# Attention over the context: scaled keys, a negated row maximum, and row sums half a slot later

## The chip, the cores and the metric

One core of one Trainium2 chip runs the whole program. The metric is the device time of one execution in microseconds. An execution was also recorded by the hardware profiler; its rows are used below.

## What is computed

A transformer block with an encoder over a short context (2 x 77 tokens) and a decoder over 2 x 2048 tokens in blocks, width 512, 16 heads of 32. What matters here is the decoder's attention over the encoder's output:

```python
q = (xq @ wq.T + bq).reshape(Bq, Tq, H, hd).transpose(0, 2, 1, 3)
k = (xkv @ wk.T + bk).reshape(Bq, Tk, H, hd).transpose(0, 2, 1, 3)
v = (xkv @ wv.T + bv).reshape(Bq, Tk, H, hd).transpose(0, 2, 1, 3)
scores = jnp.einsum('bhqd,bhkd->bhqk', q, k) / jnp.sqrt(jnp.asarray(hd, xq.dtype))
scores = scores + bias[None]
attn = jax.nn.softmax(scores, axis=-1)
out = jnp.einsum('bhqk,bhkd->bhqd', attn, v)
```

The bias depends on the distance of the positions alone and is constant beyond 127, so for most query rows it drops out of the softmax.

## The kernel before

The program runs its stages one after the other: encoder, decoder projections, attention of the decoder over itself, its output with the next projection, `cross_attention` (the attention over the context), feed-forward. Each stage is a block of five instruction streams, one for each engine, ordered by semaphores; the next block starts when all have ended.

In `cross_attention` the queries are worked in chunks: 8 groups of 512 tokens (`GW`) times 4 sets of 4 heads (`KC`, `HC`) are `NQ` = 32 chunks, each of `TT` = 4 blocks of 128 queries. A block has 4 x 77 = 308 columns of scores. Block `n` goes through these steps:

- `score(n)` on TensorE, three matmuls into one of three PSUM banks (`sps`). It waits until the exponentials of block n-3 have freed the bank.
- `shift(n)` on VectorE (L1279): if the block is near (`near(n)`: the first two blocks in the chunks of the first group of each batch, 16 in all) it adds the bias (L1287), then takes the maximum over the 77 columns of each head (L1289, into `mx`) and multiplies by -SCALE (L1291, into `ng`).
- `exponent(n)` on ScalarE (L1243): four activations, one for each head, exp(SCALE * score + ng), into `pq` (L1248).
- `sums(n)` on VectorE (L1293): the row sums into `den` (L1296); `inverse(n)` (L1298) takes the reciprocal for two blocks (L1301).
- GpSimd multiplies `pq` by the reciprocal (L1162).
- For the chunk: `turn` on TensorE transposes `pq` into two PSUM banks (L1198), `evacuate` on ScalarE copies them out (L1256), `values` multiplies with the values (L1208), `high` (ScalarE, L1262) and `low` (VectorE, L1306) split the result in two parts, `project` on TensorE multiplies with the output weights (L1222), and `residual` on VectorE adds `y` (L1311), to which GpSimd has added the bias row (L1169).

The order is written out by hand as slots from -2 to 36. In slot q the engines do the scores, maxima, exponentials and sums of chunk q+2 (`LEAD`), the transposes of chunk q, the values of chunk q-1, `high` and `low` of chunk q-2, and the projection of token block q-5 (`LAG`). A slot has two halves, with two blocks and two transposed heads in each. VectorE's half is: maxima of two blocks, sums of the same two, their reciprocal. ScalarE's half is: two evacuations, then the exponentials of two blocks. In slots 0 to 15 GpSimd also splits a block of weights for a later stage in two parts (L431, L436, L438).

The keys come from the encoder. There, for each of four chunks `m`, TensorE leaves a projection in PSUM and VectorE writes its high part (`ckh`, L405) and what is left (`ckl`, L407). `G` holds the rows of the relative bias; each has its constant far value taken off and is divided by SCALE (L331).

Of the kernel before, what the change touches and what calls it, by code (L numbers as in the profile page):

```python
# [30 lines left out]
P = 128  # L31
# [85 lines left out]
def encoder(k, io, dr, ident, weights):  # L117

    nc = k.nc
    with k:  # L120
# [34 lines left out]
        s = k.sems("enc", "x wqkv wo wff1 wff2 wkv cols vrow grow gx0 gx1 g gs bias gx ones idz id mm xc"  # L155
                          " sq var sd rs hs h qk v st sc mx sub ex sum rec nrm pt ptc ot otc x1 hid mem ck cl cv one out")

# [160 lines left out]
        def _(dve):  # L318
# [10 lines left out]
            dve.wait_ge(s["gx0"], 2)  # L329
            for i, f in ((0, far_sa), (1, far_sa), (2, far_ca), (3, far_ca)):  # L330
                dve.tensor_scalar(G[:, i, :], G[:, i, :], f[:, 0:1], 1.0 / SCALE, ALU.subtract, ALU.mult).then_inc(s["gx1"], 1)  # L331
            dve.wait_ge(s["gx1"], 4)
# [3 lines left out]
            for n, (kind, m) in enumerate(UNITS):  # L336
# [65 lines left out]
                elif kind == "ck":  # L402
                    ready(n)
                    bk = cols[:, BCK + m:BCK + m + 1]
                    dve.tensor_scalar(ckh[:, m, :], out[:, 0:SE], bk, None, ALU.add).then_inc(s["ck"], 1)  # L405
                    dve.wait_ge(s["ck"], m + 1)
                    dve.scalar_tensor_tensor(ckl[:, m, :], out[:, 0:SE], bk, raw(ckh[:, m, :]),  # L407
                                             ALU.add, ALU.subtract).then_inc(s["cl"], 1)
                else:
# [641 lines left out]
def cross_attention(k, io, dr, ident, w, split, src, dst):  # L1051
# [7 lines left out]
    with k:  # L1059
# [3 lines left out]
        ub = k.sb("ca_ub", [P, 2, H, S])  # L1063
        mx = k.sb("ca_mx", [P, PB * TT, HC])
        ng = k.sb("ca_ng", [P, PB * TT, HC])
# [11 lines left out]
        ops = [k.ps(f"ca_p{i}", [P, D]) for i in range(2)]  # L1077
        s = k.sems("ca", "zero0 zero1 key0 key1 val near brow q0 q1 q2 score biased max shift exp sum inverse normal"
                         " turned copied value high low product added done y0 y1 y2 y3 st0 st1 st2 st3")
# [5 lines left out]
        def chunk(q):  # L1085
            return q // KC, q % KC, q // KC // GB

        def blocks(q):
            return [q * TT + i for i in range(TT)]

# [58 lines left out]
        def _(pool):  # L1149
# [7 lines left out]
            for q in slots():  # L1157
                if has(q + LEAD):
                    for n in blocks(q + LEAD):
                        pool.wait_ge(s["inverse"], n // 2 + 1)  # L1160
                        r = n % (PB * TT)
                        pool.tensor_tensor(pq[:, r], pq[:, r], inv[:, r].unsqueeze(2).to_broadcast([P, HC, S]),  # L1162
                                           ALU.mult).then_inc(s["normal"], 1)
# [78 lines left out]
        def _(act):  # L1242
            def exponent(n):  # L1243
# [3 lines left out]
                for j in range(HC):  # L1247
                    last = act.activation(pq[:, r, j, :], sps[n % 3][:, j * S:(j + 1) * S], ACT.Exp,  # L1248
                                          bias=ng[:, r, j:j + 1], scale=SCALE)
                last.then_inc(s["exp"], 1)  # L1250
# [25 lines left out]
        def _(dve):  # L1276
            dve.memset(raw(kd[0][:]), 0.0).then_inc(s["zero0"], 1)

            def shift(n):  # L1279
# [3 lines left out]
                if near(n):  # L1283
# [4 lines left out]
                    dve.wait_ge(s["biased"], nears(n))  # L1288
                dve.tensor_reduce(mx[:, r], tile, AX_X, ALU.max).then_inc(s["max"], 1)  # L1289
                dve.wait_ge(s["max"], n + 1)  # L1290
                dve.tensor_scalar(ng[:, r], mx[:, r], -SCALE, None, ALU.mult).then_inc(s["shift"], 1)  # L1291

# [20 lines left out]
            for q in slots():  # L1313
                if has(q - 2):
                    low(q - 2)
                for half in range(2):
                    if has(q + LEAD):
                        n = TT * (q + LEAD) + 2 * half
                        shift(n)
                        shift(n + 1)  # L1320
                        sums(n)
                        sums(n + 1)
                        inverse(n)
                    if half == 0 and has(q - LAG - 1, NE):
# [481 lines left out]
```

## Time and profile before

| | us |
|---|---|
| median of three runs | 3056.75 |
| lowest and highest | 3056.3, 3058.85 |
| the profiled execution, its own time | 3056.01 |
| its span, first to last instruction | 3054.2 |
| first bias addition of the stage, start | 1968.80 |
| last residual of the stage, start | 2267.24 |

The page of a profile shows for each engine the time it was busy, the span in slices, and a chain of work followed back from the end. Here the core is mostly busy with matmuls, and the stage in question covers about a tenth of the span. Busy shares say little of it: engines wait for each other, so it is read by slots, by waits and by the timeline.

### The profile page before, as it was taken

The page shows a single profiled execution, that of the slowest core. Times are in us where ns is not written, and L with a number is a line of the kernel's source. Part 1 is how long each engine was busy: PE and PEld are TensorE (multiplying, and loading weights), DVE is VectorE, ACT ScalarE, POOL GpSimd, SP SyncE. Part 2 cuts the span into 40 slices and gives each one's busy share as a digit, 9 for nine tenths or more (in the row PEclk, how much of TensorE's full clock was granted, in tenths as well). Part 3 has the DMA queues.
Part 4 walks back from the last instruction along what each step waited for, and adds up shares of the span by engine and source line. Part 5 has one row for each costly group of instructions (what it writes and reads, how often), then busy time and mean ns, then how long its engine had stood idle before and what let it go on. Part 6 is the DMA issues. An engine that isn't in the chain of part 4 may idle for free. (4 is left out here: it accounts for less than half of the span.)

```text
span 3054.2 us, 42604 instructions
## 1 busy us (share of the span) xinstructions
PE 2765.9 (91%) x12704; PEld 1815.9 (59%) x12704; DVE 1662.1 (54%) x3992; ACT 1241.8 (41%) x2630; POOL 373.6 (12%) x459
## 2 busy tenths in 40 slices
PE   5689978999999999999999499588969999999998
PEld 4578864444444444444443377456647777777777
DVE  4244537777777777777774466378842221222211
ACT  0032322555555555555555243276733222222222
POOL 0300002000000000000000111266447000000000
PEclk7899996999999999999999799799989999999999
DMA  9344444222222222222220775534331000000000
GB/s 286 74 164 167 180 162 119 63 64 64 65 64 65 64 65 64 65 66 64 64 64 8 177 234 192 167 114 136 125 113 47 28 28 28 1 27 27 28 14 14
DMA packets 133924, 271.63 MB, mean 89 GB/s; under 512 B 33875, under 2 KB 54867, under 8 KB 128192
## 3 DMA queue, kind: packets, MB, share of 16 engines
q1 hardware_dynamic: 128896, 254.17, 28.6%
q0 software_dynamic: 4800, 14.68, 1.6%
q8 instruction: 111, 1.82, 0.3%
q14 instruction: 117, 0.96, 0.1%
HBM read 174.39 MB, written 99.98 MB: 90 GB/s over the span
## 5 line engine op out<-in xcount | busy, mean ns | idle before, releaser
L969 ACT ACTIVATE sa_pr<-sa_st 128x512 f32<-128x512 f32 (+3 forms) x1280 | 612.1, 532 | 566.4 <-DVE sa_st L1032 324.4
L937 PE MATMUL sa_ov<-sa_pr,sa_v 128*33 128x512 f32 (+3 forms) x2560 | 537.7, 541 | 0.0
L1018 DVE TENSOR_REDUCE sa_part<-sa_mp 128x1 f32<-128x512 f32 (+3 forms) x768 | 411.4, 583 | 120.4 <-PE sa_mp L918 119.5
L928 PE MATMUL sa_st<-sa_q,sa_k 97*128 97x512 f32 (+3 forms) x1280 | 439.8, 413 | 23.8 <-ACT sa_pr L969 13.2
L928 PEld LDWEIGHTS sa_st<-sa_q,sa_k 97*128 97x128 f32 x1280 | 216.9, 190 | 323.1 <-ACT sa_pr L969 206.1
L918 PE MATMUL sa_mp<-sa_k,sa_q 96*128 96x512 f32 (+3 forms) x1280 | 373.5, 386 | 25.2 <-DVE sa_mp L996 19.7
L1015 DVE CUSTOM_DVE_ANT_0 sa_mp<-sa_mp,sa_ub 128x512 f32<-128x512 f32 (+3 forms) x512 | 318.0, 664 | 76.7 <-PE sa_mp L918 71.8
L1676 DVE TENSOR_TENSOR ff_hl<-ff_hf,ff_hh 128x512 fp32r<-128x512 f32 x128 | 93.9, 734 | 479.4 <-ACT ff_hh L1658 479.4
L105 PE MATMUL ff_f<-ff_ln_hi,ff_w 128*128 128x512 f32 x1024 | 344.0, 397 | 2.9 <-DVE ff_ln_lo L529 2.9
L1621 PE MATMUL ff_o<-ff_w,ff_hh 128*128 128x512 f32 x1024 | 323.8, 397 | 3.1 <-DVE ff_hl L1676 3.1
L918 PEld LDWEIGHTS sa_mp<-sa_k,sa_q 96*128 96x128 f32 x1280 | 233.2, 194 | 96.0 <-DVE sa_part L1018 24.4
L1655 ACT ACTIVATE ff_hf<-ff_f,ff_b 128x512 f32<-128x512 f32 x128 | 88.0, 687 | 471.6 <-PE ff_f L105 471.5
L937 PEld LDWEIGHTS sa_ov<-sa_pr,sa_v 128*33 128x33 f32 x2560 | 122.2, 111 | 258.0 <-issue 206.6
L1032 DVE TENSOR_TENSOR sa_st<-sa_st,sa_tb 128x256 f32<-128x256 f32 (+1 forms) x608 | 206.9, 381 | 81.6 <-PE sa_st L928 80.2
L105 PEld LDWEIGHTS ff_f<-ff_ln_hi,ff_w 128*128 128x128 f32 x1024 | 193.5, 189 | 50.5 <-DVE ff_ln_lo L529 3.3
L1621 PEld LDWEIGHTS ff_o<-ff_w,ff_hh 128*128 128x128 f32 x1024 | 191.2, 188 | 51.3 <-DVE ff_hl L1676 3.4
L1428 POOL TENSOR_TENSOR sao_y<-sao_y,sao_brow 128x512 f32<-128x512 f32 x32 | 42.3, 1354 | 1363.5 <-DMA sao_y<-in_x 1363.5
L105 PE MATMUL ff_f<-ff_ln_lo,ff_w 128*128 128x512 f32 x512 | 203.0, 396 | 0.0
L1621 PE MATMUL ff_o<-ff_w,ff_hl 128*128 128x512 f32 x512 | 202.2, 395 | 0.0
L105 PE MATMUL qkv_ring<-ln_hi,qkv_w 128*128 128x512 f32 x512 | 165.0, 397 | 3.4 <-DVE ln_lo L529 3.4
L1248 ACT ACTIVATE ca_pq<-ca_s,ca_ng 128x77 f32<-128x77 f32 x512 | 120.8, 335 | 96.4 <-DVE ca_ng L1291 95.8
L1188 PE MATMUL ca_s<-ca_k,ca_q 128*128 128x308 f32 x384 | 85.6, 346 | 47.9 <-ACT ca_pq L1248 30.6
(186 smaller groups left out, 3361.3 us busy)
## 6 DMA issues: line engine op xcount, KB each, us to landing
sa_q<-scratch_q SPq DMA_DIRECT2D x192, 128.0 KB, 4.4
sa_k<-scratch_k SPq DMA_DIRECT2D x192, 128.0 KB, 4.6
scratch_q<-qkv_qst SPq DMA_DIRECT2D x32, 512.0 KB, 2.8
scratch_k<-qkv_qst SPq DMA_DIRECT2D x32, 512.0 KB, 2.8
scratch_q<-sao_qst SPq DMA_DIRECT2D x32, 512.0 KB, 2.9
ca_q<-scratch_q SPq DMA_DIRECT2D x32, 512.0 KB, 4.1
scratch_v<-qkv_vst SPq DMA_DIRECT2D x8, 1056.0 KB, 5.2
sa_v<-scratch_v SPq DMA_DIRECT2D x16, 528.0 KB, 6.5
```

The lines of the kernel that those rows point to most:

```text
L105: last = pe.matmul(out, s, m, start=(k == 0), stop=(k == n - 1))
L918: pe.matmul(mp[a % 2][:, h, 0:w], qs[n.par][rows, h, qb * P:(qb + 1) * P], ks[n.par][rows, h, k0:k0 + w], start=True, stop=True).then_inc( ...
L928: pe.matmul(st[bank(u, h)][:, 0:w], ks[n.par][:, h, kb * P:(kb + 1) * P], qs[n.par][:, h, g * GW + c0:(g + 1) * GW], start=True, stop=True ...
L937: last = pe.matmul(ov[64 * h:64 * h + VW, c0:GW], vs[n.par][:, kb, h, :], pr[:, u % 4, h, 0:GW - c0], start=(u in opens), stop=(u in ends))
L969: act.activation(pr[:, u % 4, h, 0:w], st[bank(u, h)][:, 0:w], ACT.Exp, scale=SCALE).then_inc(s["exp"], 1)
L1015: dve.tensor_tensor_reduce(tile, tile, ub[n.par][:, h, GW - w:GW], 1.0, NEG, ALU.add, ALU.max, to)\
L1018: dve.tensor_reduce(to, tile, AX_X, ALU.max).then_inc(s["red"], 1)
L1032: dve.tensor_tensor(tile, tile, tb[n.par][:, h, t0:t0 + w], ALU.add).then_inc(s["bias"], 1)
L1248: last = act.activation(pq[:, r, j, :], sps[n % 3][:, j * S:(j + 1) * S], ACT.Exp, bias=ng[:, r, j:j + 1], scale=SCALE)
L1621: last = pe.matmul(ops[i][:], a[:, f % 2, t], b[:, f, :], start=(f == 0 and n == 0), stop=(f == FC - 1 and n == 2))
L1655: act.activation(hf[:, f % 2, :], fps[f % 2][:], ACT.Relu, bias=b1[:, f:f + 1]).then_inc(s["relu"], 1)
L1676: dve.tensor_tensor(hl[:, f % 2, :], hf[:, f % 2, :], raw(hh[:, f % 2, :]), ALU.subtract)\
```

## The change

- In the encoder the projected key plus its bias is multiplied by SCALE in full precision into `sq` (a tile that is free by then), copied into `ckh`, and the difference goes to `ckl`. There is one semaphore more, `cs`.
- The bias rows for the attention over the context are no longer divided by SCALE.
- In `cross_attention` the scores are thus scaled already. The maximum is written with its sign turned (`negate=True`) straight into `ng`; `mx`, its multiplication and its semaphore go. The exponential has no scale.
- VectorE takes the sums and the reciprocal of the two blocks of the half before, and GpSimd's loop over blocks is moved by two blocks with it.

```diff
-            for i, f in ((0, far_sa), (1, far_sa), (2, far_ca), (3, far_ca)):
-                dve.tensor_scalar(G[:, i, :], G[:, i, :], f[:, 0:1], 1.0 / SCALE, ALU.subtract, ALU.mult).then_inc(s["gx1"], 1)
+            for i, f, unit in ((0, far_sa, 1.0 / SCALE), (1, far_sa, 1.0 / SCALE), (2, far_ca, 1.0), (3, far_ca, 1.0)):
+                dve.tensor_scalar(G[:, i, :], G[:, i, :], f[:, 0:1], unit, ALU.subtract, ALU.mult).then_inc(s["gx1"], 1)
...
-                    dve.tensor_scalar(ckh[:, m, :], out[:, 0:SE], bk, None, ALU.add).then_inc(s["ck"], 1)
+                    dve.tensor_scalar(sq[:, m, :], out[:, 0:SE], bk, SCALE, ALU.add, ALU.mult).then_inc(s["cs"], 1)
+                    dve.wait_ge(s["cs"], m + 1)
+                    dve.tensor_copy(ckh[:, m, :], sq[:, m, :]).then_inc(s["ck"], 1)
                     dve.wait_ge(s["ck"], m + 1)
-                    dve.scalar_tensor_tensor(ckl[:, m, :], out[:, 0:SE], bk, raw(ckh[:, m, :]),
-                                             ALU.add, ALU.subtract).then_inc(s["cl"], 1)
+                    dve.tensor_tensor(ckl[:, m, :], sq[:, m, :], raw(ckh[:, m, :]), ALU.subtract).then_inc(s["cl"], 1)
...
-                if has(q + LEAD):
-                    for n in blocks(q + LEAD):
+                for n in range(TT * (q + LEAD) - 2, TT * (q + LEAD) + 2):
+                    if has(n, TT * NQ):
                         pool.wait_ge(s["inverse"], n // 2 + 1)
...
                     last = act.activation(pq[:, r, j, :], sps[n % 3][:, j * S:(j + 1) * S], ACT.Exp,
-                                          bias=ng[:, r, j:j + 1], scale=SCALE)
+                                          bias=ng[:, r, j:j + 1])
...
-                dve.tensor_reduce(mx[:, r], tile, AX_X, ALU.max).then_inc(s["max"], 1)
-                dve.wait_ge(s["max"], n + 1)
-                dve.tensor_scalar(ng[:, r], mx[:, r], -SCALE, None, ALU.mult).then_inc(s["shift"], 1)
+                dve.tensor_reduce(ng[:, r], tile, AX_X, ALU.max, negate=True).then_inc(s["shift"], 1)
...
                 for half in range(2):
-                    if has(q + LEAD):
-                        n = TT * (q + LEAD) + 2 * half
+                    n = TT * (q + LEAD) + 2 * half
+                    if has(n, TT * NQ):
                         shift(n)
                         shift(n + 1)
-                        sums(n)
-                        sums(n + 1)
-                        inverse(n)
+                    if has(n - 2, TT * NQ):
+                        sums(n - 2)
+                        sums(n - 1)
+                        inverse(n - 2)
```

## Rows read from the trace of the kernel before

**Rows 1.** The page, its first line.

```profile
span 3054.2 us, 42604 instructions
```

**Rows 2.** Timeline, end of the stage: start us, us, engine, line, operation, tiles, count.

```profile
2238.81 1.10 PE L1198 MATMUL ca_t<-ident,ca_pq 128*77 128x128 f32 x8
...
2267.24 0.69 DVE L1311 TENSOR_TENSOR ca_y<-ca_p,ca_y 128x512 f32<-128x512 f32 x1 [2.06 <-PE ca_p L1222]
```

**Rows 3.** Busy us by stretches: start:end, length, each engine, clock, DMA.

```profile
1968.80:1999.58 30.78, 19.60 (x93) 14.90 (x93) 24.03 (x64) 19.58 (x74) 13.20 (x18) 0.72 0.56 149
1999.58:2031.21 31.63, 24.54 (x151) 17.22 (x152) 23.79 (x61) 24.54 (x85) 21.77 (x29) 0.94 0.34 100
2031.21:2099.23 68.02, 62.71 (x393) 46.76 (x392) 54.87 (x130) 49.34 (x169) 50.81 (x64) 1.00 0.46 144
2099.23:2138.66 39.43, 33.21 (x197) 24.28 (x196) 32.31 (x74) 24.66 (x85) 22.50 (x28) 0.96 0.38 121
2138.66:2240.98 102.32, 92.74 (x573) 67.73 (x571) 81.71 (x194) 74.03 (x253) 47.41 (x60) 1.00 0.35 114
```

**Rows 4.** Waits from 1960 to 2260: who for whom, us, times, longest.

```profile
POOL ca_pq L1162 <- DVE ca_inv L1301: 115.3, 55, 3.0
ACT ca_pq L1248 <- DVE ca_ng L1291: 95.8, 89, 18.1
DVE ca_den L1296 <- ACT ca_pq L1248: 47.5, 99, 0.7
```

**Rows 5.** Groups of instructions, 1950 to 2275: busy us, mean ns, idle before.

```profile
L1291 DVE TENSOR_SCALAR ca_ng<-ca_mx 128x4 f32<-128x4 f32 x128 | 60.0, 469 | 4.4
L1289 DVE TENSOR_REDUCE ca_mx<-ca_s 128x4 f32<-128x308 f32 x128 | 59.7, 466 | 1.4 <-PE ca_s L1188 0.8
```

**Rows 6.** Timeline of half a slot, VectorE, ScalarE and GpSimd.

```profile
2058.19 1.29 POOL L1169 TENSOR_TENSOR ca_y<-ca_y,ca_brow 128x512 f32<-128x512 f32 x1
...
2058.68 0.83 DVE L1291 TENSOR_SCALAR ca_ng<-ca_mx 128x4 f32<-128x4 f32 x1
...
2059.54 0.97 ACT L1248 ACTIVATE ca_pq<-ca_s,ca_ng 128x77 f32<-128x77 f32 x4 [0.27 <-DVE ca_ng L1291]
...
2060.54 0.47 DVE L1296 TENSOR_REDUCE ca_den<-ca_pq 128x4 f32<-128x308 f32 x1 [0.67 <-ACT ca_pq L1248]
```

**Rows 7.** Timeline of the encoder: GpSimd, and VectorE around the keys.

```profile
14.50 0.93 DVE L356 TENSOR_SCALAR enc_hT<-enc_xc,enc_cols 128x154 f32<-128x154 f32 x4
...
114.43 0.99 POOL L438 TENSOR_TENSOR qkv_w<-qkv_w_stage,qkv_w 128x384 fp32r<-128x384 f32 x1
...
128.83 0.38 DVE L407 SCALAR_TENSOR_TENSOR enc_ckl<-enc_ring,enc_cols,enc_ckh 128x154 fp32r<-128x154 f32 x1
...
129.88 0.38 DVE L407 SCALAR_TENSOR_TENSOR enc_ckl<-enc_ring,enc_cols,enc_ckh 128x154 fp32r<-128x154 f32 x1
...
132.96 0.09 DVE L412 MEMSET enc_sc<- 77x32 f32 x1 [2.70 <-PE enc_ring L299]
```

**Rows 8.** Timeline of TensorE, a stretch without waits.

```profile
2134.87 1.06 PE L1208 MATMUL ca_o<-ca_pt,ca_v 77*32 77x512 f32 x8
2135.87 1.10 PE L1198 MATMUL ca_t<-ident,ca_pq 128*77 128x128 f32 x8
2136.72 1.16 PE L1188 MATMUL ca_s<-ca_k,ca_q 128*128 128x308 f32 x6
2137.72 0.63 PE L1222 MATMUL ca_p<-ca_wo,ca_oh 128*128 128x512 f32 x2
...
2139.10 1.03 PE L1198 MATMUL ca_t<-ident,ca_pq 128*77 128x128 f32 x8
```

**Rows 9.** Timeline of ScalarE, a stretch without waits inside.

```profile
2153.19 1.84 ACT L1248 ACTIVATE ca_pq<-ca_s,ca_ng 128x77 f32<-128x77 f32 x8 [1.28 <-DVE ca_ng L1291]
2154.87 0.65 ACT L1262 ACTIVATE ca_oh<-ca_o 128x512 fp32r<-128x512 f32 x1
2155.35 1.11 ACT L1256 ACTIVATE ca_pt<-ca_t 77x512 f32<-77x512 f32 x2
```

More of the change, by code:

```diff
@@ L155, in encoder @@
         s = k.sems("enc", "x wqkv wo wff1 wff2 wkv cols vrow grow gx0 gx1 g gs bias gx ones idz id mm xc"
-                          " sq var sd rs hs h qk v st sc mx sub ex sum rec nrm pt ptc ot otc x1 hid mem ck cl cv one out")
+                          " sq var sd rs hs h qk v st sc mx sub ex sum rec nrm pt ptc ot otc x1 hid mem cs ck cl cv one out")
         N1S, N1B, N2S, N2B, BQK = 0, KC, 2 * KC, 3 * KC, 4 * KC
@@ L1063, in cross_attention @@
         ub = k.sb("ca_ub", [P, 2, H, S])
-        mx = k.sb("ca_mx", [P, PB * TT, HC])
         ng = k.sb("ca_ng", [P, PB * TT, HC])
@@ L1077, in cross_attention @@
         ops = [k.ps(f"ca_p{i}", [P, D]) for i in range(2)]
-        s = k.sems("ca", "zero0 zero1 key0 key1 val near brow q0 q1 q2 score biased max shift exp sum inverse normal"
+        s = k.sems("ca", "zero0 zero1 key0 key1 val near brow q0 q1 q2 score biased shift exp sum inverse normal"
                          " turned copied value high low product added done y0 y1 y2 y3 st0 st1 st2 st3")
@@ L1086, in chunk @@
             return q // KC, q % KC, q // KC // GB
-        def blocks(q):
-            return [q * TT + i for i in range(TT)]
         def near(n):
```

## Prediction

> **What bounds the kernel now.** The profiled execution took 3056.0 us, 1.8 us of them outside its span of 3054.2 us [rows 1]; the three runs have a median of 3056.75, so I add the change to 3056.0 and take the 0.7 between them as noise. The change touches the encoder (one place, near 130 us) and the whole attention over the context, so I looked first at where that stage lies. Its four engines stop at 2267.9, when the last residual ends, and the next stage starts only behind the last stores and the block's end [rows 2]. Nothing of the next stage overlaps it: what this stage saves comes off the end, one for one.
>
> Next I cut the stage into its slots, at each slot's first VectorE instruction, and asked for the busy times [rows 3]. In the 12 slots from 2138.66 (slots 18 to 29, every kind of work present) one slot lasts 102.32 / 12 = 8.53 us, and no engine is full: PE 7.7 of 8.53 with the tails of its matmuls counted, VectorE 6.8, ScalarE 6.2, GpSimd 4.0. Slots 6 to 13 take 8.50, the four with two biased blocks each (14 to 17) 9.86. An idle share on all engines with a steady period means a loop that goes through several of them, and the waits name it: ScalarE waits 95.8 us for `ca_ng`, VectorE 47.5 us for `ca_pq` [rows 4]. The timeline shows one turn: the negated maximum is written, ScalarE starts its exponentials 0.03 us later, VectorE's sum waits for them (0.67 us idle in front of it) while the next maxima stand queued behind that sum [rows 6]. VectorE and ScalarE take turns; half a slot costs two maxima, the exponentials of the second block, and its sum.
>
> **The change part by part.**
> *The multiplication by -SCALE goes* (128 instructions at L1291). Its mean is 469 ns, as much as a maximum over 308 columns (466 ns), though it handles 4 columns [rows 5]. The timeline says why: one lasts 0.83 us, and ends within 0.03 us of the GpSimd instruction that began before it [rows 6]. So 60.0 us of VectorE go, and the stretched ones sit right in the loop. The maximum has the same length of about 0.47 everywhere, beside GpSimd work or not, so I take the negated one at 0.47. If the turned sign cost a second pass it would be 0.94, and nothing in the trace bounds it below 0.47 from another form of reduction, so I keep 0 and +0.47 as ends and take 0, the row of the same shape.
> *The sums half a slot later.* `sums(n-2)` now wait for exponentials that ran in the previous half. The wait of 47.5 us goes, and maxima no longer queue behind it. What is put off with them is GpSimd's normalisation: its first pair of a slot now belongs to the next chunk, which the transposes need one slot later instead of two.
> *ScalarE's scale argument* goes from the exponential: no instruction fewer, cost nothing. GpSimd's loop runs over the same 128 blocks.
> *The encoder*: per chunk one scaled bias addition, a copy into the high half and a subtraction, instead of two instructions at 0.38. An SBUF instruction of 154 columns costs 0.93 / 4 = 0.23 us there, so a chunk costs VectorE some 0.2 us more; TensorE needs 1.05 us for a chunk (129.88 - 128.83), more than the 1.0 that VectorE then takes. The last chunk ends about 0.2 later than 130.26, and the next VectorE work comes at 132.96: covered [rows 7]. The key stores start 0.2 later, and the value stores that end the stage wait for VectorE's work behind 132.96, so SyncE's queue is not held up either. Without that cover it would be 4 x 0.2 = 0.8 us.
> A rule that speaks against this part: the Trainium skill, page "SBUF — State Buffer", section "Who interferes with whom", says that a VectorE copy in a two-port mode, and a VectorE instruction with two SBUF inputs, block on a GpSimd instruction that reads SBUF; both kinds are new here. The trace has GpSimd's last instruction there end at 115.4, and the first key chunk at 129.88 - 0.4 - 3 x 1.05 = 126.3 [rows 7], so by the rule too the sum stays. The same section says that a reduction never contends, which no row here contradicts.
> The mask rows get factor 1.0 in place of 1/SCALE: same instruction.
>
> *What is late next.* With the loop gone each engine needs per full slot:
> - TensorE: from starts to starts, values 1.00, eight transposes 0.85, six score matmuls 1.00, six of the projection 1.38 [rows 8]; a slot has one of the first and two of each other: 1.00 + 1.70 + 2.00 + 2.76 = 7.46.
> - ScalarE: eight exponentials 1.68, `high` 0.48, two evacuations about 1.05 [rows 9]: 3.36 + 0.48 + 2.10 = 5.9.
> - VectorE: 54.87 / 8 = 6.86 busy now, less 4 x 0.469: 5.0 [rows 3, 5].
> - GpSimd: 50.81 / 8 = 6.35 while it still splits weights, 4.0 later [rows 3].
>
> So TensorE, if no wait enters it. I laid one slot out at 7.46. TensorE starts at 0. `high` runs from 0.1, the first two evacuations to 1.7. A block's scores are there 0.66 after their first matmul (1.16 - 0.50), so the first block at 1.55; its maximum is done at 2.05, its exponentials run to 3.1, those of the second to 3.9. Sums and reciprocal are through at 3.8, the residual at 4.4. Evacuations three and four run 3.8 to 4.9, score blocks three and four are written at 4.7 and 5.2, their exponentials end at 6.2 and 7.1, and the next `high` can start at 7.55. Every operand of TensorE is there at least 0.5 us ahead. In a slot with two biased blocks two additions of 0.5 come into the first half, and ScalarE ends at 7.6 with nothing to spare: 7.55. Slots 2 to 4 have no projection (TensorE 4.7), there ScalarE bounds at 5.9 to 6.0. In slots -2 to 1 VectorE has 4 maxima, 4 sums, 2 additions and reciprocals, 5.3; with ScalarE's evacuations in slots 0 and 1 and TensorE's clock at 0.72 in that stretch [rows 3], I take 23 for the four.
>
> | slots | before | after |
> |---|---|---|
> | -2 to 1 | 30.8 | 23.0 |
> | 2 to 5 | 31.6 | 3 x 6.0 + 7.5 = 25.5 |
> | 6 to 13 | 68.0 | 8 x 7.46 = 59.7 |
> | 14 to 17 | 39.4 | 4 x 7.55 = 30.2 |
> | 18 to 29 | 102.3 | 12 x 7.46 = 89.5 |
> | sum | 272.2 | 227.9 |
>
> 44.3 us. One correction: TensorE now runs 2.2 us ahead of VectorE when the scores are used up (its slot 30 begins at 2238.81, VectorE's at 2240.98 [rows 2, 3]), after the change 0.8 ahead, so 1.4 goes back. The rest, the 28.4 us from 2238.81 to 2267.24 with transposes, projections and stores, is paced by TensorE already and stays. 44.3 - 1.4 = 43: **3056 - 43 = 3013 us**.
>
> **The rivals.**
> *GpSimd becomes the bound while it splits weights* (slots 4 to 15). From the second reciprocal of a slot (6.9) come a pair, the residual's bias, a weight block and the next pair, 2 x 1.36 + 1.28 + 2.6 = 6.6: done at 13.5, needed at 2 x 7.46 = 14.9. A weight or `y` block landing 1.4 us late on that route eats the slack; if the slots fall back to 8.5, 12 x 1.04 = 12.5 of the gain is gone: 3026. For it: GpSimd would be 85% busy. Against: it waits 115 us for the reciprocals now [rows 4], and hardly for data.
> *Some of the round trip stays* (a maximum twice as dear, or ScalarE just not reaching its end): 0.45 on 24 slots is 11 us: 3024.
> *TensorE's clock falls in slots 0 to 4*, where it has 4.7 us of work in 6.0. At half the clock the work is 9.4: 3.4 more on three or four slots, 3025. The trace has the clock at 0.94 over slots 2 to 5 with TensorE busy 24.5 of 31.6 [rows 3], so I think it unlikely. The Trainium skill, page "TensorE: Matmul & The Clock Gate", Part 4, says that transposes do not count as TensorE work in the same way, which speaks for this rival; the same rows, with 1.00 in the full slots, do not bear it out.
> *Slower*: the put-off normalisation stands in TensorE's way each slot. If a pair had to be ready in the slot in which its reciprocal is made, one slot would need 6.9 + 6.6 = 13.5 us instead of 8.5 in slots 0 to 15, 16 x 5 = 80 us against some 20 us saved in the others: 3116. It decides once GpSimd's route from reciprocal to next pair takes more than two slots of 8.5, 17.0, against 13.5 by the rows: 3.5 us late, in every slot.
> *No effect*: the exponentials and TensorE pace each other by the three score banks. A bank's turn is a score 0.7, a maximum 0.5, four exponentials 1.0: 2.2 us for three blocks, while four blocks have 7.46. Hardly possible: 3056.
>
> **How the numbers follow.** 0.70 for 3013 (its own range 3004 to 3018: TensorE at 7.2 a slot, if score matmuls keep a closer pace than 1.00, gives 5 us, a quicker opening 3 more; 0.2 us more on a slot costs 5). 0.10 for GpSimd, 0.09 for the remaining round trip, 0.05 for the clock, 0.03 slower, 0.03 no effect. The range has to reach the three partial cases: 3004 to 3028. Faster by over 0.2% (6 us, about what a measurement can tell here): 0.94; within it 0.03; slower 0.03.
>
> **What would show it.** Period of slots 18 to 29 at 7.4 to 7.5 with TensorE never idle for `ca_pq`; no VectorE wait in front of `ca_den`; ScalarE's waits for the negated maximum short and spread; the maximum still 0.47 us. GpSimd as bound would show as transposes waiting for GpSimd's `ca_pq` before 2100 only. The encoder's value stores should start at the same moment. I am wrong in the main if TensorE's work in a slot is not 7.46 when packed, or if full slots show a new wait of TensorE.

## The result, and the profile after

| | median, us | runs, us | profiled execution | its span |
|---|---|---|---|---|
| before | 3056.53 | 3055.81 to 3058.85 (4) | 3056.0 | 3054.2 |
| after | 3010.91 | 3008.96 to 3011.65 (4) | 3011.65 | 3009.9 |

The ratio is 0.9849, with a 95% interval of 0.9835 to 0.9863: 1.5% faster, 2 us below the predicted 3013 and inside its range. The span is shorter by 44.3 us.

The stretches of [rows 3] again, cut at the same instructions in the kernel after (start:end, length, busy us of PE, PEld, VectorE, ScalarE and GpSimd with their instructions, granted clock, DMA share, GB/s). The sixth line is the tail from the first instruction of slot 30 to the start of the last residual, the seventh the feed-forward part to the end of the span:

```profile
1968.98:1991.34 22.36, 17.64 (x93) 13.83 (x93) 17.22 (x45) 18.86 (x74) 13.61 (x20) 0.79 0.74 206
1991.34:2016.89 25.55, 21.86 (x150) 15.45 (x150) 16.94 (x44) 24.03 (x85) 21.85 (x30) 1.00 0.42 124
2016.89:2075.94 59.05, 59.05 (x387) 45.56 (x385) 39.97 (x96) 50.34 (x169) 50.70 (x65) 1.00 0.54 171
2075.94:2105.38 29.44, 29.44 (x195) 22.79 (x193) 23.19 (x57) 25.20 (x85) 22.22 (x28) 1.00 0.49 153
2105.38:2193.74 88.36, 88.36 (x579) 68.33 (x577) 59.94 (x145) 75.34 (x253) 47.73 (x62) 1.00 0.42 133
2193.74:2222.62 28.88, 27.39 (x136) 19.66 (x133) 8.17 (x15) 5.99 (x11) 10.10 (x9) 0.94 0.32 105
2228.43:3009.90 781.47, 740.84 (x3200) 592.57 (x3200) 179.49 (x304) 213.66 (x329) 100.02 (x128) 0.98 0.08 28
```

From slot 6 to slot 29 the length of a stretch and PE's busy time are the same number: 59.05, 29.44, 88.36. In [rows 3] PE had 62.7 of 68.0 and 92.7 of 102.3 there. A full slot lasts 7.36 us in place of 8.53. That PE's busy time in slots 18 to 29 fell from 92.7 to 88.4 for the same work comes from how the profile models the ends of matmuls: a run of them that stands behind a wait reads longer than the same run packed. Busy time alone therefore doesn't prove that PE is full; its waits do better. From 2016 to 2194 of the kernel after the view of TensorE's waits has no line at all, where the kernel before had two from 2031 to 2241:

```profile
PE ca_s L1188 <- ACT ca_pq L1248: 12.5, 15, 1.9
PE ca_p L1222 <- DVE ca_ol L1306: 8.2, 6, 1.5
```

The waits of the stage, 1960 to 2230 (who for whom, us, times, longest), to be read against [rows 4]:

```profile
POOL ca_pq L1159 <- DVE ca_inv L1296: 67.8, 52, 3.0
DVE ca_ol L1301 <- ACT ca_oh L1259: 55.3, 32, 4.4
ACT ca_pq L1245 <- DVE ca_ng L1286: 36.0, 53, 17.5
```

ScalarE's wait for the negated maximum fell from 95.8 to 36.0, and 17.5 of what is left is the first one, at the stage's start. VectorE's 47.5 us in front of `ca_den` are gone. It idles now in front of `ca_ol` (55.3), which costs nothing in the full slots, since PE waits for nothing there. The groups of VectorE (busy us, mean ns, idle before), against [rows 5]:

```profile
L1286 DVE TENSOR_REDUCE ca_ng<-ca_s 128x4 f32<-128x308 f32 x128 | 57.6, 475 | 17.9 <-PE ca_s L1185 15.1
L1291 DVE TENSOR_REDUCE ca_den<-ca_pq 128x4 f32<-128x308 f32 x128 | 54.1, 464 | 0.0
```

One reduction of 475 ns does what 466 + 469 did, and the sum has no idle time ahead of it. Half a slot on the timeline of after (start, us, engine, operation, count), against [rows 6]:

```profile
2047.18 0.91 DVE L1286 TENSOR_REDUCE ca_ng<-ca_s 128x4 f32<-128x308 f32 x2
...
2047.70 1.83 ACT L1245 ACTIVATE ca_pq<-ca_s,ca_ng 128x77 f32<-128x77 f32 x8 [0.30 <-DVE ca_ng L1286]
...
2048.01 0.84 DVE L1291 TENSOR_REDUCE ca_den<-ca_pq 128x4 f32<-128x308 f32 x2
...
2048.89 0.20 DVE L1296 RECIPROCAL ca_inv<-ca_den 128x8 f32<-128x8 f32 x1
```

Two maxima, two sums and the reciprocal run without a gap, and the eight exponentials in one row beside them: the sums read the exponentials of the half before, so neither engine stops for the other but for the 0.30 us until the first maximum of a half is there.

### The profile page after: what moved, and what is told of

Its sections match the earlier page's. It is cut to its first block and busy times, and to the rows that moved or that the text cites. A ratio compares the mean times of both kernels' runs of the same rounds, so it can differ in the third digit from the quotient of the medians.

```text
span 3009.9 us, 42480 instructions
## 1 busy us (share of the span) xinstructions
PE 2752.3 (91%) x12704; PEld 1812.9 (60%) x12704; DVE 1606.2 (53%) x3868; ACT 1242.8 (41%) x2630; POOL 372.6 (12%) x459
## 5 line engine op out<-in xcount | busy, mean ns | idle before, releaser
L919 PEld LDWEIGHTS sa_mp<-sa_k,sa_q 96*128 96x128 f32 x1280 | 233.5, 194 | 94.2 <-DVE sa_part L1019 23.8
L105 PEld LDWEIGHTS qkv_ring<-ln_hi,qkv_w 128*128 128x128 f32 x512 | 97.3, 190 | 23.3 <-DVE ln_lo L530 3.3
```

What stands on the lines that cost most here:

```text
L105: last = pe.matmul(out, s, m, start=(k == 0), stop=(k == n - 1))
L919: pe.matmul(mp[a % 2][:, h, 0:w], qs[n.par][rows, h, qb * P:(qb + 1) * P], ks[n.par][rows, h, k0:k0 + w], start=True, stop=True).then_inc( ...
```

## The experiments

Each ratio is against runs of the kernel before in the same job on the same chip. The first job has e1 to e4 (before: 3055.27), the second e5 to e8 (before: 3056.96), the third the f runs (before: 3053.48), and each interval is 95%. Jobs differ by up to 3.5 us in their kernel before, so kernels of different jobs are compared by ratios. The expectations are in microseconds beside the 3056.53 of the result above, so a miss of 3 us can be the job's. Where I compare stretches of one profile each, the stage runs from the first bias addition (for before and after 1968.80 and 1968.98) to the start of the last residual: 298.4 us before, 253.6 after.

### The parts of the change alone

**e1**: the change with the sums, the reciprocal and GpSimd's normalisation at their old place, so that only the multiplication is gone (GpSimd's loop is put back likewise).

```diff
                     if has(n, TT * NQ):
                         shift(n)
                         shift(n + 1)
-                    if has(n - 2, TT * NQ):
-                        sums(n - 2)
-                        sums(n - 1)
-                        inverse(n - 2)
+                        sums(n)
+                        sums(n + 1)
+                        inverse(n)
```

> The changed kernel with the sums and reciprocals back in their own half slot: scaled keys and negated maximum alone. Theory (the multiplication, stretched by GpSimd, stands in the loop): half a slot is maximum 0.5, exponentials of two blocks to 2.3, sum and reciprocal 0.65, high/low or residual 0.6, together 3.55, so 7.1 a slot, less than TensorE's 7.46; full slots come out at TensorE's pace, only slots with biased blocks and the first seven stay longer: about 3020 us. Rival (the order of sums and maxima was the loss): little changes, 3045 or more.

Measured: 3011.89, ratio 0.9858 (0.9841 to 0.9874). Its wait in front of the sums, and its slots 18 to 29:

```profile
DVE ca_den L1291 <- ACT ca_pq L1245: 60.9, 120, 0.7
```

```profile
2113.04:2200.89 87.85, 87.85 (x574) 67.82 (x573) 61.45 (x145) 74.81 (x253) 47.54 (x60) 1.00 0.41 133
```

The wait of VectorE is even longer than before (60.9 against 47.5 us), and PE is full all the same, at 7.32 us a slot (7.1 in slots 18 and 19, in which VectorE catches up after the biased ones, and 7.35 to 7.39 from slot 20 on). Once the stretched multiplication is out of the loop, the loop is shorter than PE's work, and the sums' place no longer matters in a full slot. My 3020 was 8 us too high (see the section on the prediction), and the rival's 3045 and more fell.

**e2**: the other half. Before, with only the sums, reciprocal and normalisation moved; the multiplication stays.

```diff
                 for half in range(2):
-                    if has(q + LEAD):
-                        n = TT * (q + LEAD) + 2 * half
+                    n = TT * (q + LEAD) + 2 * half
+                    if has(n, TT * NQ):
                         shift(n)
                         shift(n + 1)
-                        sums(n)
-                        sums(n + 1)
-                        inverse(n)
+                    if has(n - 2, TT * NQ):
+                        sums(n - 2)
+                        sums(n - 1)
+                        inverse(n - 2)
```

> The kernel before with only the sums, the reciprocals and GpSimd's loop moved by two blocks; the multiplication by -SCALE stays. VectorE keeps 6.9 us of work in a slot, ScalarE starts later in each half. Theory: some 0.3 us over TensorE's pace in full slots, 0.9 in the others: about 3027. If the order alone is the cause of the gain: 3011 to 3015. If the multiplication alone: 3050 or more.

Measured: 3019.07, ratio 0.9884 (0.9868 to 0.9901). The multiplication in its groups, and slots 18 to 29:

```profile
L1291 DVE TENSOR_SCALAR ca_ng<-ca_mx 128x4 f32<-128x4 f32 x128 | 47.8, 374 | 4.4
```

```profile
2113.39:2201.53 88.14, 88.08 (x573) 67.77 (x573) 74.85 (x192) 73.30 (x253) 47.79 (x61) 1.00 0.40 132
```

The same picture from the other side: the multiplication still takes 47.8 us, VectorE has 74.85 of the 88.14, and PE is full. Either half alone is enough in slots 18 to 29. They differ from the whole change where PE has slack or VectorE has more to do. Against after, e1 loses in slots -2 to 4 and 14 to 17 together 6.4 us, by (26.04 + 19.50 + 30.97) less (22.36 + 18.28 + 29.44); for e2 the same difference is (25.55 + 19.95 + 32.80) less 70.08 = 8.2 us, and its slots 6 to 13, where GpSimd also splits weights, take 59.98 against 59.05. The tails of e1 and e2 are 1.6 and 1.5 us shorter than that of after (27.25 and 27.35 against 28.88). That is not their edit: it is TensorE's clock, as the section on the prediction shows. The expectation of e2, 8 us too high as well, had put 0.3 us on every full slot; slots 18 to 29 show none of it.

### What stretches the multiplication

The prediction read from [rows 6] that a multiplication of 4 columns lasts until a GpSimd instruction beside it ends. **e3** leaves order and number of instructions as they were before, and changes one thing only: the maximum goes into four spare columns of the scores' own PSUM bank, so that the multiplication reads PSUM and not SBUF.

```diff
-                dve.tensor_reduce(mx[:, r], tile, AX_X, ALU.max).then_inc(s["max"], 1)
+                mxp = sps[n % 3][:, 320:320 + HC]
+                dve.tensor_reduce(mxp, tile, AX_X, ALU.max).then_inc(s["max"], 1)
                 dve.wait_ge(s["max"], n + 1)
-                dve.tensor_scalar(ng[:, r], mx[:, r], -SCALE, None, ALU.mult).then_inc(s["shift"], 1)
+                dve.tensor_scalar(ng[:, r], mxp, -SCALE, None, ALU.mult).then_inc(s["shift"], 1)
```

> The kernel before, nothing moved and nothing removed; the maximum is written to four unused columns of its own PSUM bank, so that the multiplication reads PSUM and not SBUF. If the stretched multiplications come from VectorE and GpSimd sharing a way into SBUF, all 128 take some 0.2 us, half a slot falls from 4.25 to about 3.75 and the time to about 3025. If their length has another cause: 3056.

Measured: 3026.49, ratio 0.9907 (0.9891 to 0.9924). The view by tiles gives count, shortest/median/longest ns, and first and last start. First the kernel before, then e3:

```profile
L1291 DVE TENSOR_SCALAR ca_ng<-ca_mx x128: 170/475/1208, 1969.8 to 2238.9; 128x4 f32<-128x4 f32 x128
```

```profile
L1292 DVE TENSOR_SCALAR ca_ng<-ca_s x128: 160/162/166, 1971.2 to 2208.3; 128x4 f32<-128x4 f32 x128
```

All 128 take 160 to 166 ns, though 111 of them begin while GpSimd is busy, and on the timeline of e3 one of them runs its 0.17 us inside a GpSimd addition of 1.29:

```profile
2050.85 1.29 POOL L1169 TENSOR_TENSOR ca_y<-ca_y,ca_brow 128x512 f32<-128x512 f32 x1
...
2051.03 0.17 DVE L1292 TENSOR_SCALAR ca_ng<-ca_s 128x4 f32<-128x4 f32 x1
```

The trace of the kernel before says the same, instruction by instruction. The 107 multiplications that began while a GpSimd instruction ran took 225 to 1208 ns, and 104 of them ended within 0.06 us of the end of a GpSimd instruction; the 21 that began with GpSimd idle took 170 to 172. So a slower read from SBUF is no rival explanation: without GpSimd beside it the SBUF form costs 170 ns for the 162 from PSUM.

So of the 60.0 us some 39 (60.0 less 128 x 0.162) were time in which VectorE stood behind GpSimd, and in that form alone the stage lasts 268.8, 29.6 less than before. The Trainium skill states both halves of this. Its page "SBUF — State Buffer", section "Who interferes with whom", has the scalar form of VectorE's instructions able to take a mode in which it contends with GpSimd, and reductions never; this trace agrees, with up to 1208 ns for the one, and 426 to 479 ns for each of the 256 reductions of the kernel before. Its page "VectorE: DVE Perf Modes", section "Why PSUM operands drop a tier", says that this mode takes both of VectorE's read ports into SBUF, so that an operand in PSUM rules it out; the 162 ns above agree.

**e4**: e2 and e3 together, so that neither the encoder nor the sign is touched.

> The kernel before with both: sums half a slot later, and the maximum in PSUM; scale and multiplication stay. VectorE has 5.7 us a slot. Theory: TensorE's pace in all full slots, 3012 to 3018; what is left of the multiplication is worth nothing to some 4 us. Rival (the instruction count itself matters): 3025.

Measured: 3012.40, ratio 0.9863 (0.9846 to 0.9879), slots 18 to 29 in 88.18. Its interval overlaps that of the change (0.9835 to 0.9863). A version without any new arithmetic reaches the same place in full slots, since PE sets it. Its stage lasts 256.7 us against 253.6, all of it in slots -2 to 4 and 14 to 17, too little to tell in the medians.

### What bounds now

**e5**: the change, with a second negated maximum per block into a tile that nobody reads. This puts 60 us back on VectorE, in the loop and ahead of the exponentials (the tile is declared beside the others).

```diff
+                dve.tensor_reduce(spare[:, r], tile, AX_X, ALU.max, negate=True)
                 dve.tensor_reduce(ng[:, r], tile, AX_X, ALU.max, negate=True).then_inc(s["shift"], 1)
```

> The changed kernel with every maximum taken twice, the first into a spare tile: 128 x 0.47 = 60 us of VectorE put back, with no GpSimd in it. Theory (TensorE bounds, VectorE has 2.4 us free in a slot): 7.0 us of VectorE in 7.4, 0.5 us later for ScalarE; full slots +0.1, slots with biased blocks and the first seven +0.5: 3013 to 3020. Rival (VectorE still in the pace): 3040 to 3070.

Measured: 3013.26, ratio 0.9860 (0.9843 to 0.9876). The group of the added instruction, then slots 18 to 29 and 14 to 17:

```profile
L1287 DVE TENSOR_REDUCE ca_spare<-ca_s 128x4 f32<-128x308 f32 x128 | 60.1, 470 | 3.2 <-PE ca_s L1186 0.7
```

```profile
2110.15:2197.76 87.61, 87.61 (x572) 67.51 (x571) 76.20 (x192) 74.45 (x253) 47.79 (x62) 1.00 0.42 133
...
2077.97:2110.15 32.18, 31.08 (x201) 23.64 (x199) 29.06 (x73) 24.70 (x85) 22.30 (x28) 1.00 0.47 148
```

60.1 us of VectorE cost nothing in full slots (7.30 a slot, 7.35 to 7.40 from slot 20 on) and 5.1 in the stage (258.7 against 253.6), 2.7 of it in slots 14 to 17, where VectorE has 29.06 of 32.18. Against f1 below, the change again with a tail like that of e5, it is 6.1. VectorE is not the bound, and a maximum of twice the price, one of the prediction's rivals, would have taken nothing from the gain in the full slots.

**e6**: the change without the products of the rounded activation (`oh`) with the low part of the weights, four of twelve projection matmuls a slot. The output lacks that part, so its time counts only as a measure of PE.

```diff
-                    for x, (a, ww) in enumerate(((oh, wo_h), (oh, wo_l), (ol, wo_h))):
+                    for x, (a, ww) in enumerate(((oh, wo_h), (ol, wo_h))):
...
-                                         start=(c == 0 and x == 0), stop=(c == KC - 1 and x == 2))
+                                         start=(c == 0 and x == 0), stop=(c == KC - 1 and x == 1))
```

> The changed kernel without the product of the high part and the low weights in the output projection: four of twelve matmuls of 0.23 us go in each of 32 slots, and the output lacks that part. Theory (TensorE sets the pace): 32 x 0.92 = 29 us, less what ScalarE keeps in slots with biased blocks: 2982 to 2988. Rival (a round trip through the other engines still sets it): above 3005.

Measured: 2978.28, ratio 0.9747 (0.9731 to 0.9764). Slots 18 to 29:

```profile
2091.48:2168.24 76.76, 76.76 (x526) 58.76 (x525) 59.53 (x144) 73.25 (x253) 47.68 (x61) 1.00 0.47 152
```

The slot goes from 7.36 to 6.40: 0.96 for four matmuls, which at 1.39 us for six (the timeline of after, below) are 0.93 of PE's work. The time follows PE's work one for one, which it could not do with another engine as the bound. The median is 4 us below the range I expected; the tail alone went from 28.88 to 20.89 us, and 1.6 of that is the clock. The next bound is in sight: ScalarE has 73.25 of 76.76.

**e7**: the change with two more GpSimd additions of 128x512 in each of the slots 4 to 15, where GpSimd also splits weights.

```diff
+                if 4 <= q < 16:
+                    for _ in range(2):
+                        pool.tensor_tensor(idle[:, _], brow[:], brow[:], ALU.add).then_inc(s["idle"], 1)
```

> The changed kernel with two more additions of 128x512 on GpSimd in slots 4 to 15, ahead of the weight block (1.28 us each). GpSimd has 6.6 + 2.6 = 9.2 us in a slot of 7.4. Theory (its route has two slots of time): the slots go to GpSimd's own pace of 9.1, 12 x 1.7 = 21 us less the slack of 1.4: about 3030. Rival (the put-off pair is needed within the slot in which its reciprocal is made): TensorE stands by the whole addition and more, above 3060.

Measured: 3016.45, ratio 0.9868 (0.9852 to 0.9885). Slots 6 to 13, and the group of what was added:

```profile
2015.93:2082.01 66.08, 61.93 (x383) 45.30 (x380) 39.94 (x96) 50.50 (x168) 65.39 (x80) 1.00 0.48 153
```

```profile
L1171 POOL TENSOR_TENSOR ca_idle<-ca_brow 128x512 f32<-128x512 f32 x24 | 24.4, 1033 | 0.0
```

GpSimd is now full (65.39 of 66.08), PE is not, and a slot lasts 8.26 us. Slot 6 still has TensorE's pace, 7.39; slots 7 to 13 last 8.32 to 8.47, and GpSimd's own 6.34 (50.70 / 8) with two additions at 1.03 makes 8.40. I had expected 3030, from slots of 9.1, which is 0.7 too high: the additions cost 1.03 and not 1.28, and the rest of GpSimd's slot 6.34 and not 6.6. The stage grew by 9.4 us only (263.0 against 253.6). The slots never lasted longer than GpSimd's work, so the route from reciprocal to transpose costs nothing of its own; the theory behind the slower rival, that a pair must be ready within one slot, has no support. The ratio, 0.9868 against 0.9849, shows less than the 9.4 us of this one profile (0.3%), and its interval overlaps that of the change. That a GpSimd at 86% (50.70 of 59.05) leaves PE full in the kernel after is what refutes the first rival.

### The start of the stage

In after VectorE's first addition waits 15.05 us for the bias table, and comes 8.5 us after PE's first score (1960.48). **e8** loads the table in four sets of heads, the first set ahead of the rest and each with its own semaphore.

```diff
-            for i in range(2):
-                sp.dma_start(ub[:, i], dr["ca_U"].ap()[:, i * P:(i + 1) * P, :].rearrange("h p j -> p h j"))\
-                  .then_inc(s["near"], 16)
+            def load_u(m):
+                hs = slice(m * HC, (m + 1) * HC)
+                for i in range(2):
+                    sp.dma_start(ub[:, i, hs], dr["ca_U"].ap()[hs, i * P:(i + 1) * P, :].rearrange("h p j -> p h j"))\
+                      .then_inc(s[f"near{m}"], 16)
+            load_u(0)
+            load_u(1)
             load_q(2)
+            load_u(2)
+            load_u(3)
...
-                    if n == 0:
-                        dve.wait_ge(s["near"], 32)
+                    if q < KC and n % TT == 0:
+                        dve.wait_ge(s[f"near{m}"], 32)
```

> The changed kernel with the bias table loaded in four sets of heads with a semaphore each, the sets of the first two chunks ahead of the third block of queries; VectorE's first addition waits for a quarter of the table. It waits 15 us for the whole one now, 6 of them after the first scores. Theory: the stage starts 3 to 4.5 us sooner: 3007. Rival (the keys or the queries land no sooner, or the later sets come late): 3011.

Measured: 3005.42, ratio 0.9833 (0.9817 to 0.9849). The first addition on the timeline of after, then on that of e8 with what waits later:

```profile
1968.98 0.49 DVE L1284 TENSOR_TENSOR ca_s<-ca_s,ca_ub 128x308 f32<-128x308 f32 x1 [15.05 <-DMA ca_ub<-scratch_ca_U]
```

```profile
1961.50 0.49 DVE L1290 TENSOR_TENSOR ca_s<-ca_s,ca_ub 128x308 f32<-128x308 f32 x1 [10.17 <-DMA ca_ub<-scratch_ca_U]
...
1979.86 1.47 PE L1191 MATMUL ca_s<-ca_k,ca_q 128*128 128x308 f32 x6 [2.00 <-DMA ca_q<-scratch_q]
```

The addition comes 3.65 us after PE's first score (1957.85), where f1 below, the change again, needs 8.4. Some is given back: slots -2 to 1 last 25.2 us and not 22.4, with 2.00 of waiting for the queries that now stand behind the table.

To see this beside the change on one chip I ran both again, **f1** (the change) and **f2** (e8), and **f3**, which has e8 with the loads of the residual's row, the first `y` and the second keys moved into slots 0 and 3, behind the queries.

```diff
-            sp.dma_start(brow[:], io["ca_bo"].partition_broadcast(P)).then_inc(s["brow"], 16)
-            for e in range(YB):
-                load_y(e)
-            load_k(1)
             for q in slots():
                 if has(q + LEAD) and has(q + LEAD + QB):
                     load_q(q + LEAD + QB)
+                if q == 0:
+                    sp.dma_start(brow[:], io["ca_bo"].partition_broadcast(P)).then_inc(s["brow"], 16)
+                    for e in range(YB):
+                        load_y(e)
+                if q == 3:
+                    load_k(1)
```

> The changed kernel, unaltered, on the chip of the next two: 3011 us within 3, slots 18 to 29 at 7.37 us each.

> The kernel with the bias table in four sets once more, to part its gain from the 4 us by which the start of this stage differs between executions. In its first trace the first addition came 4.9 us sooner after the first scores, and slots -2 to 1 took 2.9 us longer, TensorE waiting 2.0 us for the queries of chunk 3. Theory: 2 us faster than the changed kernel beside it: 3009. Rival (its first run showed the whole gain): 3005.

> The same with the loads of the bias row and of y put behind the queries of chunk 4, and the second batch's keys behind those of chunk 8. Theory (the queries of chunk 3 were late only because 24 transfers stood before them in SyncE's queue): slots -2 to 1 at 22.4 us again, the whole 4.9 us kept, 3006. Rival (bytes, not the place in the queue): no better than the kernel without it.

| | median, us | ratio (95%) | PE's first score to first addition | slots -2 to 1 |
|---|---|---|---|---|
| f1 | 3006.49 | 0.9841 (0.9828 to 0.9855) | 8.40 | 22.9 |
| f2 | 3001.82 | 0.9827 (0.9814 to 0.9840) | 3.28 | 23.8 |
| f3 | 3002.40 | 0.9829 (0.9816 to 0.9843) | 3.03 | 23.9 |

By the medians f2 is 4.7 us below f1, and the start of its one profile gives 5.12 - 0.89 = 4.2 of that, but the intervals of the ratios overlap: a version faster than the change is likely, not shown beyond doubt. All three came out below their expectations; their kernel before was 3.1 us faster than the 3056.53 of the result, and by the ratio f1 is where the change was (0.9841 and 0.9849), with slots 18 to 29 at 7.36. The gain of f2 over f1 is nearer the rival's than the 2 us of the theory.

The theory of f3 failed: slots -2 to 1 take 23.9 and not 22.4. Nor does the pair test it. f3 has no wait for queries, but in the profile of f2 TensorE doesn't wait for them either; the 2.00 us stand in e8's alone. What f3 does show is the clock. Its slot 3 lasts 7.19 us at 0.82, where f1 has 6.12 at 1.00:

```profile
1992.63:1999.82 7.19, 7.19 (x47) 5.91 (x45) 4.48 (x12) 6.17 (x22) 5.83 (x9) 0.82 0.35 95
```

The windows of f3 over the start (columns as above):

```profile
1960.00:1970.00 10.00, 6.58 (x24) 5.26 (x23) 6.24 (x16) 5.45 (x24) 6.78 (x10) 0.60 1.14 283
1970.00:1980.00 10.00, 8.35 (x38) 7.35 (x39) 6.40 (x18) 7.26 (x28) 5.29 (x8) 0.66 0.42 123
```

The granted clock of TensorE is 0.60 and 0.66 there, after a stretch in which it waited for the loads, and PE is busy 8.35 of 10 us in the second. Whether the low clock or the short waits for GpSimd's pairs hold these slots at 23.9 was not settled.

## Why the prediction came out right

**The bound, right.** TensorE was to become the only limit of a full slot and never idle for `ca_pq`: PE is busy 59.05 of 59.05, 29.44 of 29.44 and 88.36 of 88.36 us, and waits for nothing there. e5 and e6 show it by force: 60.1 us more on VectorE cost 5.1 and none in full slots, 0.93 us less on PE gave 0.96 per slot.

**The size of a slot, 0.1 too high.** The sum was 1.00 + 1.70 + 2.00 + 2.76 = 7.46, and it is 7.36. On the timeline of after, starts to starts:

```profile
2147.81 1.07 PE L1205 MATMUL ca_o<-ca_pt,ca_v 77*32 77x512 f32 x8
2148.81 1.10 PE L1195 MATMUL ca_t<-ident,ca_pq 128*77 128x128 f32 x8
2149.66 1.10 PE L1185 MATMUL ca_s<-ca_k,ca_q 128*128 128x308 f32 x6
2150.60 0.62 PE L1219 MATMUL ca_p<-ca_wo,ca_oh 128*128 128x512 f32 x2
...
2151.99 1.04 PE L1195 MATMUL ca_t<-ident,ca_pq 128*77 128x128 f32 x8
2152.78 1.09 PE L1185 MATMUL ca_s<-ca_k,ca_q 128*128 128x308 f32 x6
2153.72 0.63 PE L1219 MATMUL ca_p<-ca_wo,ca_oh 128*128 128x512 f32 x2
...
2155.20 1.07 PE L1205 MATMUL ca_o<-ca_pt,ca_v 77*32 77x512 f32 x8
```

Values 1.00 and the first projection 1.39 as predicted; six scores 0.94 and not 1.00, twice a slot, and one of the two runs of transposes 0.79 and not 0.85. The second projection, with the values behind it, takes 1.48 and not 1.38. The terms were off by -0.12, -0.06 and +0.10, and in part made up for each other; this slot lasts 7.39, the mean is 7.36. The prediction had named the score matmuls as the term that might be too high. The biased slots did not fall behind either: 29.44 / 4 = 7.36 for the 7.55 of the hand-laid slot.

**Stretch by stretch.**

| slots | predicted | after |
|---|---|---|
| -2 to 1 | 23.0 | 22.4 |
| 2 to 5 | 25.5 | 25.6 |
| 6 to 13 | 59.7 | 59.1 |
| 14 to 17 | 30.2 | 29.4 |
| 18 to 29 | 89.5 | 88.4 |
| sum | 227.9 | 224.8 |
| tail | 26.3 + 1.4 | 28.9 |

The slots gave 272.2 - 224.8 = 47.4 us for the predicted 44.3. The tail, 26.3 us before, took back 2.6 for 1.4. The step behind the 1.4 was right: TensorE begins slot 30 at 2192.97, 0.77 us ahead of VectorE, for the predicted 0.8. What the prediction had left out is that TensorE's clock may fall in the tail. Here is the matmul of after that waits in the tail, and the 6 us that follow:

```profile
2209.80 0.73 PE L1219 MATMUL ca_p<-ca_wo,ca_oh 128*128 128x512 f32 x2 [1.44 <-DVE ca_ol L1301]
```

```profile
2210.00:2216.00 6.00, 6.00 (x20) 4.80 (x20) 1.03 (x2) 0.00 (x0) 2.16 (x2) 0.72 0.35 119
```

At 0.72 these 6 us hold some 1.7 us of stretching. The wait itself is not new. The kernel before has the same one, and its clock stayed at 1.00 behind it:

```profile
2255.91 0.74 PE L1222 MATMUL ca_p<-ca_wo,ca_oh 128*128 128x512 f32 x2 [1.44 <-DVE ca_ol L1306]
```

```profile
2256.00:2262.00 6.00, 6.00 (x27) 4.91 (x28) 1.41 (x3) 0.00 (x0) 2.04 (x2) 1.00 0.49 167
```

All 13 profiles on record have this wait of 1.44 us in the tail. In after, e3, e4, e8 and f3 the clock fell behind it, and their tails last 28.5 to 28.9 us. In the other eight it stayed at 1.00; the tails of e1, e2, e5, e7, f1 and f2 last 27.3 to 27.4 (before has its 26.3, e6 with fewer matmuls 20.9). f1 is the same program as after. So 1.6 us of the 28.9 come and go from one execution to the next, and without them the tail would have taken back 1.0 for the predicted 1.4.

In the stage 47.4 - 2.6 = 44.8 were gained. Outside it, the way from the last residual's end to the next stage's first instruction went from 6.4 us to 5.1 (2223.31 to 2228.43), the feed-forward part from 779.90 to 781.47 with the same busy time of PE, and the stage began 0.2 later: 44.8 + 1.3 - 1.6 - 0.2 = 44.3, the difference of the spans. That the forecast of 43 came within 2 us is in part luck: the slots gave 3.1 us more, and the tail (1.2) and the rest of the program (0.5) took part of it back.

**The multiplication, right.** The negated maximum costs 475 ns against 466, the value taken, not a second pass. That GpSimd had stretched what went away, argued from one pair of ends in [rows 6], is shown by e3 and by 104 of 107 ends. What the prediction did not see is how the two halves of the change overlap. It priced them only together. The parts alone bring the stage from 298.4 to 257.9 (e1) and 261.0 (e2), 40.5 and 37.4 us, and both together 44.8. The expectation of e2 shows the step: it added a wait to every full slot, where the longer of loop and TensorE's work decides. That of e1 did compare the two; of its 8 us some 2 are the slot of 7.46 for 7.36, and the rest was not followed up. The loop before was 8.53, TensorE's work 7.4, so a cut of about 1.2 us in the loop should be enough. e3 comes close, but not all the way: it cut 4 x (0.469 - 0.162) = 1.23 us, and its slots 18 to 29 lasted 7.52 us, 1.01 less, with PE busy in 88.62 of 90.26. What is cut in the loop does not come off the period one for one:

```profile
2120.15:2210.41 90.26, 88.62 (x572) 67.61 (x571) 67.78 (x194) 72.33 (x253) 47.44 (x60) 1.00 0.39 129
```

**The encoder, right.** VectorE around the last key chunk in after, against [rows 7]:

```profile
129.14 0.38 DVE L405 TENSOR_SCALAR enc_sq<-enc_ring,enc_cols 128x154 f32<-128x154 f32 x1
129.55 0.24 DVE L407 CAST enc_ckh<-enc_sq 128x154 fp32r<-128x154 f32 x1
129.83 0.32 DVE L409 TENSOR_TENSOR enc_ckl<-enc_sq,enc_ckh 128x154 fp32r<-128x154 f32 x1
132.63 0.09 DVE L413 MEMSET enc_sc<- 77x32 f32 x1 [2.48 <-PE enc_ring L299]
```

The chunk costs 0.38 + 0.24 + 0.32 where it was 2 x 0.38, so 0.2 more, and 2.48 us of idle time behind the last one cover it. The value stores are issued at 136.72 (137.05 before), in both kernels 10.73 us after the first key instruction (125.99 and 126.32).

**The rivals.** GpSimd as bound: refuted by PE full in slots 6 to 13 with GpSimd at 50.7 of 59.05, and by e7, in which 2.07 us more a slot use up the slack of 7.36 - 6.34 = 1.0 and lengthen it by the rest. A round trip that stays: no, ScalarE waits 0.30 us per half slot and PE does not see it; in slots 14 to 17, where e5 has it, it costs 0.7 a slot. The clock in slots 0 to 4: in after slots 2 to 5 ran at 1.00 (1991.34 to 2016.89) with PE busy 21.86 of 25.55, and slots -2 to 1 at 0.79 against 0.72 before, so nothing was lost against the kernel before. But the 0.82 in slot 3 of f3 shows that the rival can happen, at 1.1 us for the slot. The Trainium skill's rule that transposes do not count as TensorE's busy time in the same way (page "TensorE: Matmul & The Clock Gate", Part 4) spoke for this rival. These slots do not test it, nor do the full ones that the prediction named against it: by the prediction's terms a slot without projection has 1.7 us of transposes beside 3.0 of scores and values. Slower by the put-off normalisation: in full slots no such wait shows. At the start of the stage, in slots 0 to 2, TensorE does wait for GpSimd's pairs in after, and not in the kernel before; it is the predicted mechanism, at 1.7 us in all:

```profile
PE ca_t L1195 <- POOL ca_pq L1159: 1.7, 4, 0.8
```

No effect: from slot 6 on TensorE never waits for a score bank in after. In the kernel before it did, 12.5 us in slots 6 to 29 (the first of its two lines above), as the far end of the loop.

## What to carry to other kernels

Where no engine is full and the period is steady, find the loop that goes through several engines and the engine with the most work; the gain of any cut in the loop ends at that engine's work, so two cuts that each reach it are not worth their sum (here 40.5 and 37.4 us alone, 44.8 together). Look among the instructions of such a loop for a tiny one whose mean is far above its shortest time: moving its operand from SBUF to PSUM, or folding it into its producer, can take more from the loop than its size suggests. Price what is left by starts to starts of packed runs, since a run that stands beside a wait is measured too long.

## What the runs showed of the hardware

- A VectorE multiplication of 128x4 fp32 with its operand in SBUF took 170 to 172 ns when it began with GpSimd idle (21 cases) and 225 to 1208 ns when it began beside a GpSimd instruction (107 cases); the same with its operand in PSUM took 160 to 166 in 128 of 128 cases.
- A maximum over 128x308 from PSUM costs the same with its sign turned: 475 ns against 466, and 470 in e5.
- A GpSimd addition of 128x512 took 1033 ns with one tile as both inputs (e7) and 1.28 us with two different ones.
- Behind the same wait of 1.44 us TensorE's clock fell in 5 of 13 executions (to 0.72 over 6 us in after) and stayed at 1.00 in 8. In kernels whose tail has the same matmuls it lasted 28.5 to 28.9 us with the fall and 27.3 to 27.4 without. First additions of after and f1 came at 1968.98 and 1967.33. Differences of 1 to 2 us between single profiles in these two places say nothing of an edit.
